# An S4D block and a routed feed-forward, one core: the mixer laid out by channel, its power tables expanded on GpSimd, its group outputs passed through a DRAM table

## The chip, the cores and the metric

The kernel runs on one core of a Trainium2 chip. TensorE (PE), VectorE (DVE), ScalarE (ACT), GpSimd (POOL) and SyncE (SP, which here issues DMAs) run their own instruction streams and wait for each other by semaphores. The metric is the device time of one launch in microseconds (us), as the median of several runs. A profile of one execution has its own span, from the first instruction to the last.

## The reference

All data are fp32: 8 batches of 512 tokens with 128 features, 256 mixer channels, 8 complex states for each channel.

```python
xz = einsum('bld,ed->bel', hidden, W_in);  x, z = split(xz, 2, axis=1)
x = silu(causal_depthwise_conv(x, conv_w, 4 taps) + conv_b)
A = -exp(log_A_real) + 1j * A_imag;  dtA = exp(log_dt) * A
Ct = (C_re + 1j * C_im) * (exp(dtA) - 1) / A
k = 2 * real(einsum('hn,hnl->hl', Ct, exp(dtA * t)))        # t = 0 .. 511
y = causal_convolution(x, k) + x * D                        # by FFT
h = layernorm(hidden + einsum('bhl,dh->bld', y * silu(z), W_out))
e = argmax(h @ gate_w.T + gate_b + expert_bias)             # 1 of 8 experts
out = layernorm(h + relu(h @ w1[e] + b1[e]) @ w2[e] + b2[e])  # 128 -> 512 -> 128
```

Both kernels do the long convolution in 4 chunks of 128 tokens. Inside a chunk, a channel's x is multiplied by a 128x128 Toeplitz matrix of k. From chunk to chunk, 8 complex states (16 numbers) for each channel are carried forward and multiplied by powers of exp(dtA). The 256 channels are worked through in 32 groups of 8.

## The kernel before

The program has four stages.

**Projection and tables (0 to 80 us).** The four convolution taps are folded into four copies of the input weights (`Wx`), so PE projects x with four accumulated matmuls for each chunk (L1292) and the gate input z with one (L1275). DVE adds the bias and writes x into `X`, where a channel's values lie 128 bytes apart (L881); ACT copies z into `Z` (L643). Beside this ACT and DVE build the power tables: `turnsC` and `Ctab`, made by whole-table arithmetic over 2048 columns (L982, L983, exponentials at L659, sines), and the lag tables `Btab` and `decay`. PE sums the rows of k, SP writes them to a DRAM table and reads Toeplitz matrices back. SP also fills the whole DRAM table of routed rows with empty rows in this stage (three DMAs of 2310 KB and one of 1848 KB).

**Groups (80 to 131 us).** For each of 32 groups PE convolves (L1370), sums the states that enter each chunk (L1357), transposes the output of the group before back to tokens in partitions and adds its states (L1380, L1384). ACT copies x and the PSUM results for it (L713, L719, L723), DVE masks states (L1044) and multiplies the output by the gate (L1057, straight out of PSUM into `X`). POOL multiplies `Btab` with `decay` for each group (`group_tables`, L515); of both tables it takes one group's column, and the group index is the innermost of 32, so that an input row is read at a step of 128 bytes. SP streams one 512 KB Toeplitz block per group through 8 slots (L424).

**Output projection and routing (131 to 142 us).** PE transposes the gated output (L1418), ACT copies it (L761), PE multiplies by the output weights (L1433, L1435). Then come squares and the deviation on ACT, the routing of each batch ("quad") on DVE, and the place of each token. Constants for these are written by POOL at L586 to L597. POOL then sends each tile of 128 rows to its place in the DRAM table (`dispatch`, L568).

**Experts (142 to 264 us).** 32 indirect dispatches by POOL; after the first 20 SP begins to load slots (L450); 39 expert blocks on PE (L1469, L1477, L1487), each with its weights from SP (L371), its layernorm on DVE and ACT and an indirect store by POOL (L576).

What orders the work is the written order on each engine and the semaphores; there is no planner.

## Time and profile before

| | us |
|---|---|
| time, median of 3 runs (lowest, highest) | 269.08 (268.27, 269.29) |
| span of the profiled execution | 263.8 |
| stage of projection and tables | 0 to 80 |
| stage of the groups | 80 to 131 |
| output projection up to the first dispatch | 131 to 141.9 |
| from the first dispatch to the end | 141.9 to 263.8 |

The profiled execution has no run time of its own on record, only its span. The launch's time contains the span and what lies around it: the median is 5.3 us above the span. PE is busy for 91% of the span, DVE 67%, ACT 71%, POOL 53%. These shares are means over stages with different limits, so the stages are to be read one by one.

### The profile page before, as it was taken

How to read it: one execution, taken by the hardware profiler on the slowest of the kernel's cores; microseconds unless marked ns; L12 is line 12 of the kernel's file. 1: busy time of each engine (PE TensorE's matmuls, PEld its weight loads, DVE VectorE, ACT ScalarE, POOL GpSimd, SP SyncE). 2: the span in 40 equal slices, each digit the busy share in tenths (PEclk: the TensorE clock that was granted, in tenths of full speed). 3: DMA queues.
4: the chain of work that ended last, by engine and by line, in shares of the span. 5: the costliest groups of instructions: out<-in, count | busy, mean ns of one | idle time of the engine just before them, and what ended most of it. 6: DMA issues, size and time to landing. Idle time of an engine off the chain costs nothing.

```text
span 263.8 us, 8892 instructions
## 1 busy us (share of the span) xinstructions
PE 239.2 (91%) x2763; PEld 215.1 (82%) x2764; DVE 177.0 (67%) x552; ACT 187.1 (71%) x528; POOL 139.8 (53%) x208
## 2 busy tenths in 40 slices
PE   8999979999999899999979999359989999999970
PEld 4888768888887678888869999349979999899960
DVE  1889995997218657777724878842877676566672
ACT  2999999856998778888655665207667777667740
POOL 6000000400009989999624687878746656657545
PEclk9999999999999999999999999759999999999995
DMA  7697884600399999999293221647865676677600
GB/s 232 180 313 288 346 334 150 244 0 0 105 310 332 310 279 296 308 320 302 66 361 120 93 93 41 212 92 191 220 179 172 200 210 164 203 195 208 189 34 6
DMA packets 54267, 52.06 MB, mean 197 GB/s; under 512 B 4415, under 2 KB 42817, under 8 KB 54114
## 3 DMA queue, kind: packets, MB, share of 16 engines
q1 hardware_dynamic: 51506, 46.65, 59.2%
q0 software_dynamic: 2304, 4.34, 4.6%
q10 hardware_dynamic: 432, 0.79, 0.8%
q8 instruction: 11, 0.18, 0.3%
q14 instruction: 14, 0.11, 0.1%
HBM read 38.14 MB, written 14.07 MB: 198 GB/s over the span
## 4 chain that ended last, share of the span: by engine, by line
PE 59%; DVE 10%; ACT 10%; POOL 9%; issue 6%; DMA 5%; SPq 1%; DVEq 0%; ACTq 0%; POOLq 0%
PE banks L1292 13%; PE banks L1477 9%; PE banks L1487 8%; PE banks L1370 7%; POOL dispatched_rows L568 5%; ACT BR L672 5%; PE banks L1380 5%; PE banks L1384 4%; PE banks L1275 3%; PE banks L1357 3%; PE banks L1435 2%; DMA X<-dispatched_rows 2%; POOL RE L558 1%; DMA out<-X 1%; POOL out L576 1%
## 5 line engine op out<-in xcount | busy, mean ns | idle before, releaser
L515 POOL TENSOR_TENSOR Wx<-BR,RE 128x384 f32 (+1 forms) x32 | 47.9, 1548 | 27.9 <-PE banks L1292 26.6
L1292 PE MATMUL banks<-Wx,XT 128*128 128x256 f32 x256 | 59.9, 380 | 1.7 <-ACT Z L643 1.7
L809 ACT ACTIVATE Z<-banks,BR 128x128 f32<-128x128 f32 x156 | 44.6, 368 | 18.4 <-PE banks L1477 18.3
L1292 PEld LDWEIGHTS banks<-Wx,XT 128*128 128x128 f32 x256 | 48.4, 190 | 9.0 <-issue 2.2
L576 POOL DMA_INDIRECT out<-X x39 | 38.4, 986 | 27.8 <-DVE X L1233 15.3
L1477 PE MATMUL banks<-Z 128*128 128x128 f32 x312 | 42.7, 281 | 0.4 <-ACT Z L798 0.2
L1487 PE MATMUL banks<-BR,Z 128*128 x312 | 41.1, 276 | 1.2 <-DVE X L1216 1.2
L1477 PEld LDWEIGHTS banks<-Z 128*128 128x128 f32 x312 | 39.0, 196 | 1.0 <-issue 0.5
L1487 PEld LDWEIGHTS banks<-BR,Z 128*128 128x128 f32 x312 | 37.8, 192 | 1.5 <-issue 1.5
L568 POOL DMA_INDIRECT dispatched_rows<-TR,CR x32 | 31.0, 970 | 9.3 <-POOL RE L558 9.3
L1057 DVE TENSOR_TENSOR X<-banks,Z 128x256 f32 (+1 forms) x32 | 20.4, 636 | 9.1 <-PE banks L1384 9.1
L521 POOL MEMSET RE<- 128x128 f32 x1 | 0.2, 205 | 44.0 <-DVE CR L989 44.0
L1370 PE MATMUL banks<-TR,RE 128*32 128x128 f32 x512 | 21.3, 279 | 1.4 <-issue 1.2
L1216 DVE TENSOR_TENSOR X<-banks,X 128x128 f32<-128x128 f32 x39 | 11.3, 289 | 14.9 <-PE banks L1487 13.4
L881 DVE TENSOR_TENSOR X<-banks,cbias 128x512 f32<-128x512 f32 x15 | 15.3, 1062 | 8.5 <-PE banks L1275 8.4
L1435 PE MATMUL banks<-Wx,RE 128*128 128x136 f32 x128 | 20.1, 279 | 0.0
L1370 PEld LDWEIGHTS banks<-TR,RE 128*32 128x32 f32 x512 | 12.3, 109 | 9.4 <-ACT RE L713 5.8
L798 ACT ACTIVATE Z<-banks 128x128 f32<-128x128 f32 x39 | 11.3, 289 | 10.8 <-PE banks L1469 10.3
L1275 PE MATMUL banks<-Win,XT 128*128 128x256 f32 x64 | 18.5, 381 | 0.0
L772 ACT ACTIVATE RE<-banks 128x128 f32<-128x128 f32 x32 | 8.9, 278 | 13.2 <-PE banks L1435 8.8
L558 POOL MEMSET RE<- 128x128 f32 x56 | 12.7, 226 | 9.1 <-DVE CR L1141 7.9
L1044 DVE SCALAR_TENSOR_TENSOR Win<-banks,RE,mask 128x192 f32<-128x192 f32 x32 | 13.4, 418 | 6.1 <-PE banks L1357 4.3
(220 smaller groups left out, 469.6 us busy)
## 6 DMA issues: line engine op xcount, KB each, us to landing
TR<-kernel_rows SPq DMA_DIRECT2D x32, 512.0 KB, 6.5
Z<-w SPq DMA_DIRECT2D x39, 256.0 KB, 3.1
dispatched_rows<-TR SPq DMA_DIRECT2D x3, 2310.0 KB, 8.8
X<-dispatched_rows SPq DMA_DIRECT2D x39, 66.0 KB, 2.1
XT<-hidden_t SPq DMA_DIRECT2D x10, 256.0 KB, 3.1
RE<-decay_and_turns SPq DMA_DIRECT2D x2, 1024.0 KB, 7.4
BR<-w SPq DMA_DIRECT2D x1, 2048.0 KB, 8.2
dispatched_rows<-TR SPq DMA_DIRECT2D x1, 1848.0 KB, 7.8
```

What stands on the lines that cost most here:

```text
L515: nc.gpsimd.tensor_tensor(BC[:, k, 0:LAGS, :].rearrange("p m (s r n) -> p (m s) r n", s=STRIPS, r=2), Btab[:, :, :, :, :, one].rearrange(" ...
L558: nc.gpsimd.memset(pause[:, 0:columns], 0.0).then_inc(s_pause, 1)
L568: pool.indirect_dma_start(slots_dram, bass.IndirectOffsetOnAxis(pos[:, batch, k:k + 1], 0), X1[:, batch, k, :], None).then_inc(s_sc[batch] ...
L576: pool.indirect_dma_start(out_rows, bass.IndirectOffsetOnAxis(XS[:, n % ROWS_RING, TOKEN_COL:TOKEN_COL + 1].bitcast(U32), 0), F[:, slot, : ...
L809: last = nc.scalar.activation(HT[:, j, c * P:c * P + P], bank[UP_BANKS[j]][:, c * P:c * P + P], ACT.Relu, bias=B1[:, bass.ds(experts[j] * ...
L1057: tt(group, bank[4 + k][:, 0:GH * TILES].rearrange("p (h t) -> p h t", h=GH), gates, ALU.mult).then_inc(s_yc, 1)
L1275: return mm(bank[Z_BANKS[k]][:, j * CHAN:(j + 1) * CHAN], XT[:, slot, at:at + CHUNK], Win[:, CHAN:], start=True, stop=True)
L1292: last = mm(bank[X_BANKS[k]][:, j * CHAN:(j + 1) * CHAN], XT[:, slot, at:at + CHUNK], Wx[:, tap, :], start=(tap == 0), stop=(tap == TAPS - 1))
L1370: last = mm(yt[part:part + TILES, at:at + P], xg[:, h, :], Tring[:, k, h, :], start=True, stop=True)
L1435: last = mm(projected(slot, k), GT[:, slot, k, j * P:j * P + P], Wo[:, j, :], start=False, stop=(j == 1))
L1477: last = mm(bank[UP_BANKS[m % 4]][:, c * P:c * P + P], WS[:, stage, c * P:c * P + P], XsT[:, m % DEEP, :], start=True, stop=True)
L1487: last = mm(bank[DOWN_BANKS[m % 2]][:, 0:P], HT[:, m % DEEP, c * P:c * P + P], W2[:, e, c * DM:(c + 1) * DM].rearrange("p e d -> p (e d)") ...
```

## The change

The mixer is laid out anew.

- x is projected by channel: PE makes 16 units (2 halves of 128 channels, 8 batches) of 128 channels by 512 tokens, and 16 like it for z, which ACT passes through Silu into `Z`. The taps are no longer in the weights: ACT applies the last tap and the bias (`last_tap`), DVE the other three in one instruction each (`add_taps`), PE transposes a unit (`turn_x`) and ACT writes it through Silu into `X` (`keep_x`).
- The power tables are built from 16 fine and 8 coarse angles for each channel and state. DVE, ACT and POOL make the short tables (896 columns and small ones of 32). POOL then expands them into the full 128x2048 halves of `Etab`, by two products and one sum each (`expand_half`), and makes the turning matrices (`turning`). The second product of each half goes into `products`, which lies in the upper half of `X`.
- For each four groups PE sums the local states (`sum_local`), ACT copies them, PE turns them by the lags (`turn_states`), DVE masks them; for each group PE convolves into an output bank and adds the states there as two halves of 64 rows (`add_states`). The transposes of the group output and `group_tables` are gone.
- ACT copies a group's output (`keep_y`) and sends it from its own DMA queue (`send_y`, 128 KB) into the DRAM table `rows_dram`. SP reads the table back into `Y` in three loads (`LOADS`: groups 0 to 15, 16 to 27, 28 to 31), four partitions for each group and 32 KB for each partition, so that channels lie in partitions again by chunk and batch.
- The gate is a product of `Y` and `Z` over 1024 columns for each quad: quads 0, 2, 4, 6 and 7 on DVE, 1, 3 and 5 on POOL. `Y` goes straight into the output projection; its transposes and copies are gone, and hidden states are all held, so the four late loads of them are gone.
- Toeplitz slots go from 8 to 5. The early fills of empty rows are gone; instead SP writes 8 blocks of 66 KB behind the experts' last rows, ahead of the slot loads of block 8.

The core of the diff:

```diff
-T_SLOTS = 8
...
+T_SLOTS = 5
...
+POOL_QUADS = (1, 3, 5)
+LOADS = ((0, 16), (16, 28), (28, 32))
...
+        def expand(engine, out, part, by_coarse, by_fine):
+            count = part.stop - part.start
+            shape = [P, count, COARSE, FINE]
+            return engine.tensor_tensor(
+                out.rearrange("p g (b a) -> p g b a", b=COARSE), by_coarse[:, part, :].unsqueeze(3).to_broadcast(shape),
+                by_fine[:, part, 0:FINE].unsqueeze(2).to_broadcast(shape), ALU.mult)
+
+        def gate(engine, n):
+            y, z = [a[:, n * CHUNKS:(n + 1) * CHUNKS, :, :].rearrange("p t j u -> p (t j u)") for a in (Y, Z)]
+            return engine.tensor_tensor(y, y, z, ALU.mult)
...
+            def store_rows(j):
+                sp.wait_ge(s_kx, 2 * j + 2)
+                sp.dma_start(kext[j * P:(j + 1) * P, :], Kx[:, j, :]).then_inc(s_kd[j], 16)
+                sp.wait_ge(s_kd[j], 16)
...
+            store_rows(0)
+            for g in range(T_SLOTS):
+                load_toeplitz(g)
+            store_rows(1)
+            def load_outputs(k):
+                first, end = LOADS[k]
+                for slot in range(Y_RING):
+                    sp.wait_ge(s_yd[slot], end // Y_RING * 16)
+                sp.dma_start(Y[first * 4:end * 4, :, :, :].rearrange("p t j u -> p (t j u)"), rows_dram[first * 4:end * 4, :])\
+                    .then_inc(s_yl[k], 16)
+
+            for g in range(T_SLOTS, 24):
+                load_toeplitz(g)
+            load_outputs(0)
+            for g in range(24, GROUPS):
+                load_toeplitz(g)
+            load_outputs(1)
...
+                if g == EARLY_BLOCKS - 4:
+                    sp.wait_ge(s_last, 2)
+                    sp.wait_ge(s_ends, 2)
+                    starts = table_values(sp, ends, 0, EMPTY_ROW - P) + table_values(sp, ends, 4, EMPTY_ROW - P)
+                    for downwards in range(2):
+                        wait_past(sp, s_fill, downwards * 16 * (EXPERTS // 2))
+                        for e in range(downwards, EXPERTS, 2):
+                            sp.dma_start(slots_dram[bass.ds(starts[e], P), :], empty_block).then_inc(s_fill, 16)
...
-            def group_tables(r, k):
-                g = r * 2 + k
-                wait_apart(pool, s_s, g - 1)
-                one = bass.ds(g, 1)
...
-                nc.gpsimd.tensor_tensor(
-                    BC[:, k, 0:LAGS, :].rearrange("p m (s r n) -> p (m s) r n", s=STRIPS, r=2),
-                    Btab[:, :, :, :, :, one].rearrange("p m s r n g -> p (m s) r (n g)"),
...
+            def turning(part):
+                count = (part.stop - part.start) * LAGS * 2
+                tt(Rot[:, part, :].rearrange("p g (m c) -> p (g m) c", c=FINE),
+                   turned[:, part, :, :].rearrange("p g m r -> p (g m r)").unsqueeze(2).to_broadcast([P, count, FINE]),
+                   same_state[:, :].unsqueeze(1).to_broadcast([P, count, FINE]), ALU.mult).then_inc(s_rot, 1)
+
+            def expand_half(part, ready):
+                expand(nc.gpsimd, Etab[:, part, :], part, first_coarse, cosine)
+                done(expand(nc.gpsimd, products[:, part, :], part, second_coarse, sine))
+                tt(Etab[:, part, :], Etab[:, part, :], products[:, part, :], ALU.add).then_inc(ready, 1)
+
+            pool.wait_ge(s_far, 1)
+            expand_half(slice(0, HALF), s_e0)
+            turning(slice(0, HALF))
+            expand_half(slice(HALF, GROUPS), s_e1)
+            turning(slice(HALF, GROUPS - HALF // 2))
+            turning(slice(GROUPS - HALF // 2, GROUPS))
...
-            pool.wait_ge(s_yc, GROUPS + LEAD)
+            for k in range(len(LOADS) - 1):
+                pool.wait_ge(s_yl[k], 16)
+            pool.wait_ge(s_yl[-1], 16)
+            pool.wait_ge(s_z, UNITS)
+            for n in POOL_QUADS:
+                gate(nc.gpsimd, n).then_inc(s_gp, 1)
             nc.gpsimd.memset(OH[:, :, :, 4], 0.0)
...
+            def last_tap(u):
+                j = u // BATCH
+                act.wait_ge(s_x, u + 1)
+                wait_past(act, s_xtr, u - 1)
+                nc.scalar.activation(xc[:, u % 2, :], bank[u % 2], ACT.Identity,
+                                     scale=channel[:, j, TAPS - 1:TAPS], bias=channel[:, j, TAPS:TAPS + 1]).then_inc(s_x3, 1)
+
+            def keep_x(u):
+                j, b = u // BATCH, u % BATCH
+                act.wait_ge(s_xtr, u + 1)
+                nc.scalar.activation(x_chunks[:, j * P:(j + 1) * P, b, :], bank[2][:, :].rearrange("p (k c) -> p c k", k=CHUNKS),
+                                     ACT.Silu).then_inc(s_xe, 1)
...
+            def keep_y(g):
+                act.wait_ge(s_y, g + 1)
+                wait_past(act, s_yd[g % Y_RING], g // Y_RING * 16)
+                nc.scalar.activation(YT[:, g % Y_RING, :].rearrange("p (j u) -> p j u", j=2), later_first(g),
+                                     ACT.Copy).then_inc(s_yt, 1)
+
+            def send_y(g):
+                act.wait_ge(s_yt, g + 1)
+                home = rows_dram[g * 4:g * 4 + 4, :].rearrange("h (t c) -> (h t) c", t=TILES)
+                act.dma_start(home, YT[:, g % Y_RING, :]).then_inc(s_yd[g % Y_RING], 16)
...
+            act.wait_ge(s_rot, 1)
+            keep_local(0)
+            act.wait_ge(s_e1, 1)
+            keep_x(8)
+            last_tap(10)
+            for n in range(TURNS):
+                keep_y(4 * n)
+                if n:
+                    send_y(4 * n - 1)
+                if n + 1 < TURNS:
+                    keep_local(n + 1)
+                if n == 0:
...
+            def add_taps(u):
+                j = u // BATCH
+                dve.wait_ge(s_x3, u + 1)
+                for back in range(1, TAPS):
+                    if back > 1:
+                        dve.wait_ge(s_xk, u * LAGS + back - 1)
+                    stt(xc[:, u % 2, back:], bank[u % 2][:, 0:SEQ - back], channel[:, j, TAPS - 1 - back:TAPS - back],
...
+            def gate_quad(n):
+                if n < QUADS and n not in POOL_QUADS:
+                    gate(nc.vector, n).then_inc(s_gd, 1)
+
+            for k in range(len(LOADS)):
+                dve.wait_ge(s_yl[k], 16)
+            dve.wait_ge(s_z, UNITS)
+            gate_quad(0)
+            gate_quad(2)
             dve.wait_ge(s_cconst, 2)
             dve.wait_ge(s_oc, 2)
             dve.wait_ge(s_rconst, 1)
...
+            def convolve(g):
+                halves = output_banks(g)
+                pe.wait_ge(s_t[g % T_SLOTS], (g // T_SLOTS + 1) * 16)
+                wait_past(pe, s_yt, g - 1)
+                for h in range(GH):
+                    part = h % 4 * TILES
+                    last = mm(halves[h // 4][part:part + TILES, 0:P], X[:, g * GH + h, :], Tring[:, g % T_SLOTS, h, :],
+                              start=True, stop=False)
+                last.then_inc(s_tm, 1)
+
+            def add_states(g):
+                halves = output_banks(g)
+                pe.wait_ge(s_v, g + 1)
+                for j in range(2):
+                    rows = slice(j * 64, (j + 1) * 64)
+                    last = mm(halves[j][:, 0:P], V[rows, g % V_RING, :, :].rearrange("p h t -> p (h t)"), Etab[rows, g, :],
+                              start=False, stop=True)
...
+                        mm(projected(slot, k), XT[:, batch, at], centre[:, :], start=True, stop=False)
+                        if n in POOL_QUADS:
+                            pe.wait_ge(s_gp, POOL_QUADS.index(n) + 1)
+                        else:
+                            pe.wait_ge(s_gd, n + 1 - len([q for q in POOL_QUADS if q < n]))
                         for j in range(2):
-                            last = mm(projected(slot, k), GT[:, slot, k, j * P:j * P + P], Wo[:, j, :], start=False,
-                                      stop=(j == 1))
+                            last = mm(projected(slot, k), Y[:, batch * CHUNKS + k, j, :], Wo[:, j, :],
+                                      start=False, stop=(j == 1))
```

Three places in the order of instructions, each first as it was and then as it is. Names are those of the program's buffers; some hold one thing after another (`CR` first `Etab`, `EN` first the small tables and then `YT`, `X` in its upper half first `products`).

ACT at the start of the groups, before: copies of x and of a group's results alternate, and none waits for a table.

```order
L643 ACTIVATE Z<-banks 128x2x32x8 [waits last_gates_projected]
L713 ACTIVATE RE<-X 128x256 [waits x_biased]
L738 ACTIVATE Z<-Z 128x512 [waits z_ready,silu_table_loaded]
L719 ACTIVATE Wx<-CR 128x128
L723 ACTIVATE RE<-banks 128x256 [waits toeplitz_multiplied]
L713 ACTIVATE RE<-X 128x256 [waits states_summed]
L719 ACTIVATE Wx<-CR 128x128 [waits group_done]
```

The same place on ACT after the change:

```order
L718 ACTIVATE EN<-banks 128x192 [waits local_states_summed,turning_matrices_ready]
L693 ACTIVATE X<-banks 128x128x4 [waits x_transposed,second_half_powers_ready]
L687 ACTIVATE xc<-banks,channel 128x512 [waits x_transposed,x_projected]
L724 ACTIVATE EN<-banks 128x256 [waits group_done]
L718 ACTIVATE EN<-banks 128x192 [waits local_states_summed]
L706 ACTIVATE Kx<-banks 128x127 [waits kernel_rows_summed,constants_ready]
L707 ACTIVATE Kx<-banks,channel 128x1
L712 ACTIVATE ET<-banks 128x512 [waits powers_transposed]
L724 ACTIVATE EN<-banks 128x256 [waits group_done]
L730 DMA group_outputs<-EN 128x256 [waits group_output_copied]
```

Unit 8 of x is now kept (L693) only when POOL has the second half of the powers; the first group's output (L724) and the second half of the kernel's rows (L706) stand behind it.

POOL ahead of the groups, before: constants, then a group's tables at a time.

```order
L535 MEMSET RE 128x1
L536 MEMSET RE 128x40
L538 IOTA RE 128x40x4 x2
L541 IOTA RE 128x40
L515 TENSOR_TENSOR Wx<-BR,RE 128x384 [waits state_decay_ready,state_sines_ready,projection_ready]
L515 TENSOR_TENSOR Wx<-BR,RE 128x384
```

There after the change, behind 31 small instructions:

```order
L345 TENSOR_TENSOR CR<-Y 128x2048 [waits coarse_powers_ready,state_pattern_ready,pool_step]
L345 TENSOR_TENSOR X<-Y 128x2048
L585 TENSOR_TENSOR CR<-CR,X 128x2048 [waits pool_step]
L578 TENSOR_TENSOR Rot<-EN,same_state 128x1536
L345 TENSOR_TENSOR CR<-Y 128x2048
L345 TENSOR_TENSOR X<-Y 128x2048
L585 TENSOR_TENSOR CR<-CR,X 128x2048 [waits pool_step]
L578 TENSOR_TENSOR Rot<-EN,same_state 128x768 x2
L594 MEMSET EN 128x128 [waits turning_matrices_ready]
```

The first seven of these rows stand ahead of the signal that L693 waits for on ACT.

POOL between the groups and the routing, before:

```order
L580 MEMSET Win 128x128
L583 AFFINE_SELECT Win<-Win 128x128 [waits counting_constants_ready]
L586 MEMSET RE 128x16 [waits mixer_output_copied]
L587 MEMSET RE 128x40
L589 MEMSET RE 128x8 [waits one_hot_constants_ready]
L590 MEMSET CR 128x1
L591 MEMSET CR 128x1
L592 MEMSET TR 128x32x3
```

The same place after the change:

```order
L645 MEMSET Win 128x128 [waits gates_projected,x_projected]
L648 AFFINE_SELECT Win<-Win 128x128 [waits counting_constants_ready]
L351 TENSOR_TENSOR Y<-Y,Z 128x1024 [waits outputs_loaded2,gates_ready,outputs_loaded1,outputs_loaded0]
L351 TENSOR_TENSOR Y<-Y,Z 128x1024 x2
L656 MEMSET EN 128x16
L657 MEMSET EN 128x40
L659 MEMSET EN 128x8 [waits one_hot_constants_ready]
L660 MEMSET CR 128x1
L661 MEMSET CR 128x1
L662 MEMSET TR 128x32x3
```

Three gates now stand ahead of the constants. DVE waits for these constants behind its own first two gates:

```order
L351 TENSOR_TENSOR Y<-Y,Z 128x1024 [waits outputs_loaded2,gates_ready,outputs_loaded1,outputs_loaded0]
L351 TENSOR_TENSOR Y<-Y,Z 128x1024
L1117 MEMSET rs 128x4 [waits one_hot_constants_ready,dispatch_constants_ready,counting_constants_ready]
L1119 TENSOR_SCALAR EN<-EN 128x8 [waits residual_added_to_block]
L1120 TENSOR_SCALAR CR<-EN 128x8
L1121 TENSOR_SCALAR EN<-EN 128x8
L351 TENSOR_TENSOR Y<-Y,Z 128x1024 [waits vector_step]
L1003 RECIPROCAL rs<-sd 128x4 [waits deviation_ready]
```

The routing chain of the first quad (L1003) comes behind the wait at L1117 and behind DVE's third gate.

## Rows read from the trace of the kernel before

**Rows 1.** The page's span and its chain that ended last, by engine.

```profile
span 263.8 us, 8892 instructions
...
PE 59%; DVE 10%; ACT 10%; POOL 9%; issue 6%; DMA 5%; SPq 1%; DVEq 0%; ACTq 0%; POOLq 0%
```

**Rows 2.** Busy time by stretch: PE, PEld, DVE, ACT, POOL; clock, DMA share, GB/s.

```profile
34.00:80.00 46.00, 45.56 (x264) 39.60 (x264) 31.15 (x33) 38.67 (x49) 4.06 (x17) 1.00 0.50 169
...
80.00:131.00 51.00, 49.26 (x1417) 40.10 (x1418) 35.83 (x68) 41.76 (x114) 47.50 (x34) 1.00 0.98 279
```

**Rows 3.** The chain in order of time: start, us, what.

```profile
0.82 3.00 DMA RE<-states
...
36.37 0.43 PE banks L1275 x2
...
120.78 0.57 PE banks L1370 x16
...
122.25 0.57 PE banks L1370 x16
...
142.88 0.88 PE banks L1418 x8
```

**Rows 4.** Timeline between the last group and the first dispatch.

```profile
130.43 0.60 DVE L1057 TENSOR_TENSOR X<-banks,Z 128x256 f32<-128x256 f32 x1
...
137.44 0.18 DVE L1085 RECIPROCAL rs<-sd 128x4 f32<-128x4 f32 x1 [4.39 <-ACT sd L781]
...
141.89 0.96 POOL L568 DMA_INDIRECT dispatched_rows<-TR,CR  x1 [0.50 <-POOL RE L558]
```

**Rows 5.** Instructions by form, POOL: busy and mean ns of one | idle before.

```profile
L515 POOL TENSOR_TENSOR Wx<-BR,RE 128x384 f32 x30 | 44.9, 1549 | 1.3 <-PE banks L1357 1.2
...
L499 POOL MEMSET TR<- 128x1024 f32 x1 | 1.0, 952 | 0.0
...
L497 POOL TENSOR_TENSOR mask<-mask 128x8 f32<-128x8 f32 x1 | 0.2, 200 | 0.1
```

**Rows 6.** The same view, DVE.

```profile
L881 DVE TENSOR_TENSOR X<-banks,cbias 128x512 f32<-128x512 f32 x15 | 15.3, 1062 | 8.5 <-PE banks L1275 8.4
...
L1122 DVE TENSOR_TENSOR TR<-banks,rs 128x512 f32<-128x512 f32 x8 | 5.3, 665 | 0.0
...
L1057 DVE TENSOR_TENSOR X<-banks,Z 128x256 f32 x30 | 19.1, 638 | 8.7 <-PE banks L1384 8.7
...
L983 DVE TENSOR_TENSOR BR<-BR 128x2064 f32<-128x2064 f32 x2 | 4.6, 2310 | 0.1
```

**Rows 7.** The same view, ACT.

```profile
L643 ACT ACTIVATE Z<-banks 128x512 f32<-128x512 f32 x16 | 9.1, 585 | 3.9 <-PE banks L1275 3.9
...
L723 ACT ACTIVATE RE<-banks 128x256 f32<-128x256 f32 x32 | 12.3, 384 | 5.3 <-PE banks L1370 5.0
...
L704 ACT ACT_TABLE_LOAD x1 | 1.3, 1283 | 0.0
```

**Rows 8.** DMA issues: count, KB of one, median us from issue to landing.

```profile
TR<-kernel_rows SPq DMA_DIRECT2D x32, 512.0 KB, 6.5
...
X<-dispatched_rows SPq DMA_DIRECT2D x39, 66.0 KB, 2.1
...
BR<-w SPq DMA_DIRECT2D x1, 2048.0 KB, 8.2
```

**Rows 9.** Timeline of SP's DMA queue, in the groups and among the experts.

```profile
82.30 39.89 SPq L424 DMA_DIRECT2D TR<-kernel_rows  x24
...
183.51 0.33 SPq L371 DMA_DIRECT2D Z<-w  x1
...
184.67 0.33 SPq L450 DMA_DIRECT2D X<-dispatched_rows  x1
```

**Rows 10.** Timeline among the experts, PE and POOL.

```profile
189.75 0.27 PE L1469 MATMUL banks<-ident,X 128*128 128x128 f32 x1
...
207.58 0.98 POOL L576 DMA_INDIRECT out<-X  x1 [0.79 <-POOL RE L558]
```

More of the change, by code:

```diff
@@ L194, in build @@
         cnt = late(400, 6 * KINDS).rearrange("p (i e) -> p i e", e=KINDS)
+        ends = late(344, EXPERTS, I32)
+        last_used = late(352, EXPERTS)
+        behind = late(360, EXPERTS)
         erow = EN[:, 2192:2200]
@@ L746, in _ @@
[L746 to L762 removed]
+            act.wait_ge(s_falls, 1)
@@ new lines, in _ @@
+            for i in range(6):
+                keep_z(i)
+            keep_x(0)
+            last_tap(2)
+            keep_z(6)
+            keep_z(7)
+            keep_x(1)
+            last_tap(3)
+            for i in range(8, 12):
+                keep_z(i)
+            for u in range(2, 6):
+                keep_x(u)
+                last_tap(u + 2)
+                keep_z(u + 10)
+            keep_x(6)
+            last_tap(8)
+            keep_rows(0)
+            keep_powers(0)
+            keep_powers(1)
@@ L1311, in _, with group @@
+            def group(g):
+                convolve(g)
+                add_states(g)
             pe.wait_ge(s_warm, 1)
             for j in range(WARMING):
[L1313 to L1318 removed]
```

1158 lines of the change are left out of this document (514 added, 644 removed).

## The prediction

> **What bounds the kernel now.** I read the chain that ended last first: 59% of it is PE, and no other engine has more than 10% [rows 1]. Then the busy time by stretch, because the stages differ. In 34 to 80 us PE works for 45.6 of 46 us while the DMAs are half idle: the projection, with its taps in the weights, is PE's. In 80 to 131 us PE (49.3), POOL (47.5) and the DMAs (share 0.98) are all nearly full [rows 2]; the chain runs through the convolutions at one group in 1.47 us (120.78 to 122.25) [rows 3]. A change that frees PE alone gets little there. The third place is the gap from the last group's gated output to the first dispatch, 131.03 (130.43 + 0.60) to 141.89, thus 10.86 us [rows 4]. From there to the end it is 263.8 − 141.89 = 121.9 us. So the time of the changed kernel is settled by when its first dispatch starts, if nothing behind it changes. I build that time up from zero.
>
> **To the start of the expansions.** The changed kernel gives POOL the power tables: two products and a sum of 2048 columns for each half, with a turning of 1536 between them. Ahead of them stand: the five parameter rows, landed at 3.8 [rows 3]; two exponentials, 0.5, and two small products, 0.4; DVE's angles, five passes over 896 columns, of which the two-input ones cost 2310/2064 = 1.12 ns a column [rows 6], about 4.8 with the cheaper one-input ones: 9.8. A table load for the sines, 1.28 [rows 7], and the sines, 0.9: 12.0. On DVE then some small ones, the taps of the first unit (3 × 0.7, from 665 ns for 512 columns out of PSUM [rows 6]) and two decay products, 3.0 together: 15.0. On POOL 15 small operations of about 0.27 (200 ns for 8 columns [rows 5]; these have 32) with waits between, 4.5, then the selector (256 columns) and six of 96, 3.7: the expansions start at **23.2**.
>
> **The expansions.** Up to the signal for the second half, which ACT waits for before it keeps unit 8 of x, POOL passes 6 × 2048 + 1536 = 13,824 columns. With r ns for a column this ends at 23.2 + 13.8r. No row shows POOL on a two-input operation with inputs side by side, so r is bounded. From above: L515, 1549/384 = 4.03, which reads at a step of 128 bytes. From below: the memset, 952/1024 = 0.93, which reads nothing [rows 5]. What does such a step cost? On DVE L881, which writes at that step, takes 1062 against 665 for as many columns, 1.6 times; L1057, 638 for 256 columns, is 1.9 times as dear a column [rows 6]. With 1.75, halfway, L515 without its step is 4.03/1.75 = 2.3. I take **r = 2.3**, nearer to L515 because that is the same kind of instruction: the signal at 55.0. The Trainium skill, page GPSIMD Engine Reference, § 3.1 (side-by-side cycle accounting), gives 4497 ns for such an addition of 2048 fp32 columns, against 2293 ns on DVE; the DVE figure agrees with L983's 2310 here, and no run here shows the other. By it r is 2.2 and the total 276.
>
> Is POOL what the groups wait for? Unit by unit, the x path has PE for two projections of 512 columns (0.43 for 256 [rows 3], so 0.86 each) and four transposes (0.11 each, from 0.88 for 8 [rows 3]), 2.2; DVE 2.1 and ACT three passes of 585 [rows 7]. Units 0 to 7, the early powers and local sums make it ready at 38 to 45, I take 42. So POOL is later by 13, and the whole queue behind ACT's wait is late: the first group's output, the second half of k's rows, and with these SP's Toeplitz loads from the sixth on.
>
> **From the signal to the end of the groups.** First PE's leftovers: seven transposed units, five or six projections, rows and transposes of the second half, 14.3 us, between twelve groups of 1.2 (less than the 1.47 of before, without transposes), and 3 of passing back and forth: 32 us to the end of group 11. Meanwhile the sixth Toeplitz load can go only at 5.2 behind the signal (ACT's four operations, 2.6, and the store of k's rows, 0.35 + 2.1 + issue [rows 8]). Then the DMAs lead: 39.89/24 = 1.66 us for 512 KB [rows 9], at a DMA share that was already 0.98 [rows 2]; each group now also sends 128 KB, up to 0.42 by size, of which I take 0.3 since ACT's queue fills gaps. Loads 15 to 31 are 17 × 1.96 = 33.3, the first of them lands after 6.5 [rows 8], the last group takes 2.1. Sum: 32 + 33.3 + 6.5 + 2.1 = 74: **129.0**. Bounds: 64, if the loads run at their own pace from the sixth on; 78, if sends cost in full and the ring of 5 (was 8) adds its latency.
>
> **Group outputs by way of DRAM.** Before, the last output was in place once DVE had gated it. Now: copy 0.5, two sends' issue 0.9, store 2.1 and issue 0.4, and the third load, 16 partitions of 32 KB. For that, 3.8 if the partition count doesn't matter; the nearest row, 2048 KB into 128 partitions in 8.2 [rows 8], moves half as much in each partition, so 16.4 would be the bound. I take 3.8, since only 512 KB remain when the other two loads lie behind. In all **8** to 21: landed at 137.
>
> **Gates and routing.** POOL now runs three gates of 1024 columns before it writes the constants that DVE's chain for the first quad waits for: 3.07r = 7.1. I charge them whole, because the chain of that quad stands behind that wait on DVE. Then constants 1.2, DVE's third gate 1.15 (1024 × 1.12 [rows 6]), and from the reciprocal to the dispatch as before, 141.89 − 137.44 = 4.45 [rows 4]: **6.8**. First dispatch at 137 + 7.1 + 6.8 = **150.9**, 9.0 later. What is saved (transposes, copies, and POOL's tables per group) is within these numbers: the whole is 23.2 + 74 + 8 + 6.8 + 16.9r = 112 + 16.9r, equal to 141.89 at **r = 1.77**.
>
> **The early fills go, others come.** The old fills ran beside the projection, where the DMA share was 0.50 [rows 2]: no gain. The new ones, eight DMAs of 66 KB in two waves, stand on SP before the slot of block 8: each wave has four issues of 0.33 [rows 9] and 2.1 to land [rows 8], with reads of their addresses about 8.5 together. That slot is loaded at 184.67 [rows 9] and needed when block 8 opens, 189.75 [rows 10], so 5.1 of it lies in SP's lead and 3.5 would be late. POOL's stores trail the blocks there (block 8's at 207.58 [rows 10]), and that backlog hides it: I take 0, bound 3.5.
>
> So the profiled time is 263.8 + 9.0 = 272.8, and with the 5.3 between span and median, taken as it was, **278**.
>
> **The rivals.** *POOL is fast* (the other side). If r lies near the memset, the expansions end before the x path and the groups start at 42; that is r = 1.36. The first dispatch comes at 42 + 74 + 8 + 6.8 + 4.2 = 135, 6.9 earlier: **262**; at 0.93 1.3 less, at r = 1.6 it is 266. For it: POOL's two products read inputs that repeat one value or a row of 16, with no large step. Against it: two reads and a write for each column, where the memset only writes. It decides below 1.77. Chance 0.20; near 1.77, no change, 0.07.
>
> *POOL is as slow as L515 shows.* r = 4.03: 112 + 68.1 = 180.1, 38 later, **307**. For it: the only row of its kind. Against it: the step of 128 bytes, which costs DVE 1.6 to 1.9. Chance 0.10.
>
> *Loads into few partitions are slow.* At half the rate for the 64 and 48 partitions the three loads cost about 11 more, **289**. For it: 32 KB in each partition, twice as much as in the expert weights' load that took 8.2 [rows 8]. Against it: the first two have groups to hide behind. The Trainium skill, page SBUF — State Buffer, § "Door 1: The DMA port swizzle", says that partitions 0 to 63 reach only half of the 16 ports; no row here shows it, and by its figures the loads would add an estimated 6, 284. Chance 0.13.
>
> **How the numbers follow.** The forecast has 0.50, with its own range of 272 to 287 (r from 2.0 to 2.6 is ±5, the group phase −10 to +4, of which part is shared). All slower cases: 0.50 + 0.10 + 0.13 = 0.73; faster 0.20; the same, within 0.5%, about what a measurement of this kernel can tell from no change, 0.07. The range goes down to 263, into the fast case, and up to 300, past the slow loads but short of 307.
>
> **What the changed profile would show.** POOL's L345 at 4.7 us for 2048 columns, its first near 23; ACT's L693 ended by POOL at about 55; PE waiting for ACT before that; Toeplitz loads at 1.9 to 2.0 us each afterwards; the last load landing near 137 and the first dispatch at 151, with DVE's L1117 ended by POOL; behind it 122 us. The prediction is wrong if L345 is under 3.5 us, if PE's wait at the second half ends by something else than POOL, if the Toeplitz loads keep 1.66 or less, or if the experts' part is not 122.

## The result, and the profile after

The changed kernel takes 302.09 us (299.61 to 308.17, 5 runs) against 269.08: 1.1215 times as long, 95% interval 1.1142 to 1.1289. That is slower, as forecast, but 33 us instead of 9, and 2 us beyond the range. Of a second launch of the same kernel (301.0 us) the trace is used here, because the first one was taken in a run with PE's clock lower than in the others. The run of this second trace took 300.68 us by its own time and 298.9 by its span, so only 1.8 us lies around a span; most of the 5.3 us that I put there is the distance of the profiled run of before from the median.

The page of the second trace, span and chain by engine, answers to [rows 1]:

```profile
span 298.9 us, 8238 instructions
...
PE 45%; POOL 23%; DMA 14%; issue 10%; DVE 3%; ACT 3%; SPq 2%; ACTq 0%; POOLq 0%; DVEq 0%
```

POOL, the DMAs and "issue" (nothing that the profile shows is waited for) took what PE lost. The timeline of POOL's expansions, and of ACT where it waits for them:

```profile
21.95 3.67 POOL L345 TENSOR_TENSOR CR<-Y 128x2048 f32<-128x2048 f32 x1
...
43.97 4.53 POOL L585 TENSOR_TENSOR CR<-CR,X 128x2048 f32<-128x2048 f32 x1
...
48.53 0.60 ACT L693 ACTIVATE X<-banks 128x512 f32<-128x512 f32 x1 [7.26 <-POOL CR L585]
```

They start at 22.0 and end at 48.5: 26.5 us for 13,824 columns, r = 1.92. SP's DMA queue, to be read against [rows 9]:

```profile
52.77 48.16 SPq L410 DMA_DIRECT2D TR<-kernel_rows  x19
101.11 0.60 SPq L420 DMA_DIRECT2D Y<-group_outputs  x1
102.31 23.55 SPq L410 DMA_DIRECT2D TR<-kernel_rows  x8
...
132.24 14.93 SPq L420 DMA_DIRECT2D Y<-group_outputs  x2
```

A Toeplitz load every 2.5 us (48.16/19), then 2.9 behind the first load of outputs, where it was 1.66. That pace is PE's, not the DMAs': SP waits 45.0 us in all, in 25 waits, for PE to be done with a slot, while PE waits for a Toeplitz load 1.3 us in all between the signal and the end of the groups. The DMA issues (count, KB, median us to landing), to be read against [rows 8]:

```profile
TR<-kernel_rows SPq DMA_DIRECT2D x32, 512.0 KB, 6.1
group_outputs<-EN ACTq DMA_DIRECT2D x32, 128.0 KB, 4.7
...
Y<-group_outputs SPq DMA_DIRECT2D x1, 2048.0 KB, 15.4
Y<-group_outputs SPq DMA_DIRECT2D x1, 1536.0 KB, 14.1
```

The expert weights' load of 2048 KB took 8.2 [rows 8]; the same bytes into 64 partitions take 15.4. By stretch (columns as in [rows 2]), the DMAs' share is 0.78 at 115 GB/s in 140 to 150, in which the second load ends and the third begins, where in the groups before it was 0.98 at 279:

```profile
110.00:120.00 10.00, 3.26 (x37) 2.07 (x40) 0.00 (x0) 0.76 (x2) 0.00 (x0) 0.54 0.96 263
...
140.00:150.00 10.00, 0.00 (x0) 0.00 (x0) 0.00 (x0) 0.00 (x0) 0.00 (x0) 0.50 0.78 115
```

In 110 to 120 PE works for 3.26 of 10 us. Its timeline there:

```profile
107.47 0.64 PE L1280 MATMUL banks<-TR,X 128*32 128x128 f32 x15
...
116.74 0.37 PE L1280 MATMUL banks<-TR,X 128*32 128x128 f32 x1 [8.63 <-issue]
```

PE stops for 8.6 us between the two recorded halves of one matmul of a convolution (8 matmuls leave 16 records), which is no place to wait for data. From the last group to the first dispatch, to be read against [rows 4]:

```profile
132.93 0.38 ACT L724 ACTIVATE EN<-banks 128x256 f32<-128x256 f32 x1 [1.45 <-PE banks L1289]
...
153.74 4.51 DVE L351 TENSOR_TENSOR Y<-Y,Z 128x1024 f32<-128x1024 f32 x2 [29.37 <-DMA Y<-group_outputs]
...
153.77 8.98 POOL L351 TENSOR_TENSOR Y<-Y,Z 128x1024 f32<-128x1024 f32 x3 [81.57 <-DMA Y<-group_outputs]
...
163.52 0.06 DVE L1117 MEMSET rs<- 128x4 f32 x1 [5.26 <-POOL TR L663]
163.96 1.22 DVE L351 TENSOR_TENSOR Y<-Y,Z 128x1024 f32<-128x1024 f32 x1
...
169.91 0.96 POOL L631 DMA_INDIRECT dispatched_rows<-TR,CR  x1 [0.49 <-POOL ET L621]
```

From the last copy to the landed outputs it is 20.4 us (133.3 to 153.7). The chain that ended last shows what fills them (start, us, what):

```profile
133.34 13.44 DMA group_outputs<-EN
146.85 6.70 DMA Y<-group_outputs
```

The last sends, 128 KB each, need 13.4 us beside the second load (issued at 132.2, landed at 146.3), and the third load can be issued only behind them, at 146.9. POOL's gates take 9.0, DVE's two beside them 2.26 each and the one alone 1.22; the first dispatch is at 169.9. Among the experts the late fills stand on SP's queue for 7.3 us ahead of block 8's slot:

```profile
214.84 7.32 SPq L465 DMA_DIRECT2D dispatched_rows<-ET  x8
223.14 0.35 SPq L443 DMA_DIRECT2D Z<-dispatched_rows  x1
```

### The profile page after: what moved, and what is told of

The parts are those of the page before. It is cut to its first block, busy times and chain, and to the rows that moved or that the text cites. A ratio compares the mean times of both kernels' runs of the same rounds, so it can differ in the third digit from the quotient of the medians.

```text
span 306.4 us, 8238 instructions
## 1 busy us (share of the span) xinstructions
PE 225.6 (74%) x2787; PEld 179.5 (59%) x2788; DVE 143.2 (47%) x484; ACT 129.5 (42%) x402; POOL 144.7 (47%) x221
## 4 chain that ended last, share of the span: by engine, by line
PE 37%; POOL 20%; DMA 14%; issue 13%; DVE 9%; ACT 3%; SPq 2%; ACTq 0%; POOLq 0%; DVEq 0%
PE banks L1280 8%; PE banks L1446 6%; PE banks L1289 6%; POOL out L639 4%; DMA group_outputs<-EN 4%; PE banks L1456 4%; POOL CR L585 3%; POOL Y L351 3%; PE banks L1270 3%; PE banks L1208 3%; POOL CR L345 2%; POOL X L345 2%; DMA Z<-dispatched_rows 2%; DMA XT<-hidden_t 2%; DMA Y<-group_outputs 2%
## 5 line engine op out<-in xcount | busy, mean ns | idle before, releaser
L864 ACT ACTIVATE Z<-banks,CR 128x128 f32<-128x128 f32 x156 | 44.6, 369 | 20.2 <-PE banks L1446 20.2
L639 POOL DMA_INDIRECT out<-Z x39 | 38.6, 989 | 28.7 <-POOL ET L621 12.7
L1456 PE MATMUL banks<-X,Z 128*128 x312 | 41.9, 279 | 0.0
L914 DVE SCALAR_TENSOR_TENSOR xc<-banks,channel,xc 128x511 f32<-128x511 f32 (+2 forms) x48 | 35.7, 748 | 13.1 <-ACT xc L687 11.9
L1456 PEld LDWEIGHTS banks<-X,Z 128*128 128x128 f32 x312 | 38.6, 196 | 0.0
L1408 PE MATMUL banks<-Wox,Y 128*128 128x136 f32 x128 | 23.1, 309 | 19.9 <-DVE Y L351 19.9
L1280 PE MATMUL banks<-TR,X 128*32 128x128 f32 x512 | 26.8, 338 | 10.4 <-issue 8.6
L724 ACT ACTIVATE EN<-banks 128x256 f32<-128x256 f32 x32 | 12.3, 384 | 48.9 <-PE banks L1289 36.1
L1408 PEld LDWEIGHTS banks<-Wox,Y 128*128 128x128 f32 x128 | 20.1, 218 | 20.2 <-DVE Y L351 20.2
L1289 PEld LDWEIGHTS banks<-CR,EN 64*128 64x128 f32 x128 | 13.4, 246 | 22.8 <-issue 22.0
L1289 PE MATMUL banks<-CR,EN 64*128 64x128 f32 x128 | 21.6, 412 | 3.4 <-issue 3.4
L1208 PE MATMUL banks<-XT,Win 128*128 128x512 f32 x32 | 20.7, 736 | 2.6 <-DMA XT<-hidden_t 2.6
L1147 DVE TENSOR_TENSOR Z<-banks,Z 128x128 f32<-128x128 f32 x39 | 11.4, 292 | 17.1 <-PE banks L1456 16.4
```

The source lines that it names most:

```text
L639: pool.indirect_dma_start(out_rows, bass.IndirectOffsetOnAxis(XS[:, n % ROWS_RING, TOKEN_COL:TOKEN_COL + 1].bitcast(U32), 0), F[:, slot, : ...
L724: nc.scalar.activation(YT[:, g % Y_RING, :].rearrange("p (j u) -> p j u", j=2), later_first(g), ACT.Copy).then_inc(s_yt, 1)
L864: last = nc.scalar.activation(HT[:, j, c * P:c * P + P], bank[UP_BANKS[j]][:, c * P:c * P + P], ACT.Relu, bias=B1[:, bass.ds(experts[j] * ...
L914: stt(xc[:, u % 2, back:], bank[u % 2][:, 0:SEQ - back], channel[:, j, TAPS - 1 - back:TAPS - back], xc[:, u % 2, back:], ALU.mult, ALU.ad ...
L1208: mm(bank[u % 2], Win[:, j * P:(j + 1) * P], XT[:, b, :], start=True, stop=True).then_inc(s_x, 1)
L1280: last = mm(halves[h // 4][part:part + TILES, 0:P], X[:, g * GH + h, :], Tring[:, g % T_SLOTS, h, :], start=True, stop=False)
```

## The experiments

**The kernel as it is**, for the trace above.

> The changed kernel as it is, to have a trace and a time beside the next three. First trace: powers' signal at 51.1 us, last group output 141.0, last load of the outputs landed 160.5, first dispatch 176.7. Every theory expects about 300 us and these four places within a few us (the granted clock was 0.5 to 0.7 in much of 100 to 160 us, so PE's part may vary).

Measured: 301.0 us; signal 48.5, last copy ended 133.3, outputs landed 153.7, first dispatch 169.9. The four places are 2.6 to 7.7 us earlier than in the first trace, and the distances behind the groups are the same within 1 us.

**Loads into 128 partitions.**

```diff
-sp.dma_start(Y[first * 4:end * 4, ...], rows_dram[first * 4:end * 4, :])
+count = (end - first) * 4 * 2 * TOKENS // P
+sp.dma_start(y_flat[:, first * 256:first * 256 + count],
+             bass.AP(rows_dram[:, :].tensor, first * 4 * 2 * TOKENS, [[count, P], [1, count]])).then_inc(s_yl[k], 16)
```

> The three loads of the group outputs carry the same bytes at the same places in the program, but into all 128 partitions (16, 12 and 4 KB for each) instead of 64, 48 and 16 partitions of 32 KB; the outputs come back in another layout, so the result is another one. Theory 1 (a load into few partitions moves 32 KB through each at a fixed pace, 15.6 us for the first in the first trace, and holds up the Toeplitz loads and the sends meanwhile): the first load takes some 8 us, the stall of 8.6 us of PE at 114 us goes, the last two loads take 8 instead of 19; together 15 to 20 us less than the changed kernel. Theory 2 (the DMAs simply have 8 MB more to move, however it is laid out): within 3 us of the changed kernel.

Measured: 286.16 us, 15 less, the first dispatch at 153.6. The loads in this kernel, as a DMA view:

```profile
Y<-group_outputs SPq DMA_DIRECT2D x1, 2048.0 KB, 10.8
Y<-group_outputs SPq DMA_DIRECT2D x1, 1536.0 KB, 7.0
```

PE's longest stop is 3.7 instead of 8.6, so it shrinks but does not go, and the last sends take 6.1 instead of 13.4. Theory 2 falls.

**The same rows into every second partition.**

```diff
+where = ((0, 128), (1, 97), (97, 128))[k]
-sp.dma_start(Y[first * 4:end * 4, ...], rows_dram[first * 4:end * 4, :])
+sp.dma_start(y_flat[where[0]:where[1]:2, :], rows_dram[first * 4:end * 4, :])
```

> The changed kernel with its three loads as they were (64, 48 and 16 rows of 32 KB, each into a partition of its own, at the same places in the program), only the partitions are others: every second one from 0, every second one from 1 to 95, every second one from 97, so the result is another one. What the run with 128 partitions left open is told apart. Theory 1a (32 KB through one partition is what takes the time): the first load still takes 15 us and the whole is within 2 us of the changed kernel, 299 to 301. Theory 1b (what counts is which partitions are written: the Trainium skill, page SBUF, has partitions 0 to 63 on half of the 16 ports, and partitions spread over both halves on all): the first two loads take 8 to 11 us, as with 128 partitions, and the whole is 10 to 15 us faster.

Measured: 291.66 us, 9 less (some 7 by the ratios to the kernel before, 1.095 against 1.1196), the first dispatch at 159.2:

```profile
Y<-group_outputs SPq DMA_DIRECT2D x1, 2048.0 KB, 11.0
Y<-group_outputs SPq DMA_DIRECT2D x1, 1536.0 KB, 9.2
```

Just as many partitions and 32 KB in each, and 4 to 5 us less for each of the two large loads (into 128 partitions it was 5 and 7 less): which partitions are written is what counts most. That agrees with the rule of the Trainium skill (SBUF — State Buffer, § "Door 1: The DMA port swizzle") that partitions 0 to 63 reach half of the ports. Theory 1a falls; theory 1b has the loads right and sizes the whole (10 to 15 us) a little too high. The last sends take 8.6 us here.

**The first load behind the Toeplitz loads.**

```diff
-load_outputs(0)
 for g in range(24, GROUPS): load_toeplitz(g)
+load_outputs(0)
 load_outputs(1)
```

> The first load of the group outputs is issued behind the last Toeplitz load instead of eight ahead of it; nothing else changes. Theory 1 (a load into few partitions is slow and shares nothing with the others): the groups end some 9 us earlier, without the stall of PE at 114 us, but the first load's 15 us then comes after them in part, so the first dispatch is within 4 us of the changed kernel. Theory 2 (only bytes count): also no change, but the last loads together then last 13 us for 4 MB rather than over 20.

Measured: 302.65 us, first dispatch 171.0. PE's stop of 8.6 us is 2.6 here, at the same matmul, but the last sends now wait behind the load, as ACT's timeline shows:

```profile
123.25 0.38 ACT L724 ACTIVATE EN<-banks 128x256 f32<-128x256 f32 x1 [1.11 <-DMA group_outputs<-EN]
133.13 0.38 ACT L724 ACTIVATE EN<-banks 128x256 f32<-128x256 f32 x1 [9.49 <-DMA group_outputs<-EN]
```

So the groups end no earlier (134.0), against theory 1, which had the load sharing nothing with the others: it holds up the sends, as it held up PE before. The last sends again need 14.1 us beside the second load. The three loads take 15.0, 14.1 and 6.5 us, so it is not their bytes (4 MB in 13 us, theory 2).

**Half of the second expansion left out.**

```diff
-expand_half(slice(HALF, GROUPS), s_e1)
+expand(nc.gpsimd, Etab[:, HALF:, :], slice(HALF, GROUPS), first_coarse, cosine).then_inc(s_e1, 1)
```

> POOL leaves out the second product and the sum of the second half of the powers, so the second half is half computed. The signal that ACT waits for comes 8.2 us earlier, at about 43. My step (the groups wait for POOL, and everything behind is a fixed distance from the signal): the whole is 8 us faster, less what the x path's own end (local sums copied at 42.6 in the first trace) keeps back. Rival (the groups are a matter of the DMAs, which are not full before 80 us): under 3 us faster, because DMA work from 80 us on is the same.

Measured: 300.91 us in the median (296.1 to 302.85), no difference that could be told from the spread; in the trace the first dispatch is 2.8 us earlier (167.1). POOL gives the signal at 40.7, but ACT now waits for PE:

```profile
45.85 0.60 ACT L693 ACTIVATE X<-banks 128x512 f32<-128x512 f32 x1 [4.70 <-PE banks L1223]
```

The x path is ready at 45.9, so POOL was the last by 2.7 us only (48.5 before). My step falls by size, and the rival's bound of 3 us holds; that does not show its reason, the DMAs.

**All gates on DVE** (`POOL_QUADS = ()`, gates 0 to 2 ahead of the constants).

> All eight gates on DVE (three ahead of the first quad, then one ahead of each), none on POOL; the rest is the changed kernel. In its trace POOL's three gates took 8.98 us, 3.0 each, and the two that DVE ran beside them 2.26 each, while DVE's later ones alone took 1.14. Theory 1 (DVE and POOL hold each other up when both read two operands of SBUF, and DVE's chain waits for POOL): DVE's gates take 1.14 each from the start, and from the landing of the last load to the first dispatch it is 10 us instead of 16.1; 5 to 6 us faster. Theory 2 (a gate has its price on either engine, 2.3 to 3.0): DVE's three take 6.8, and the whole is within 2 us.

Measured: 299.86 us, no difference in time; from the landing to the first dispatch it is 12.3 us instead of 16.2. All eight gates take 1.2 us on average:

```profile
L351 DVE TENSOR_TENSOR Y<-Y,Z 128x1024 f32<-128x1024 f32 x8 | 9.5, 1220 | 29.4 <-DMA Y<-group_outputs 29.4
```

So DVE's 2.26 was POOL's presence (theory 1), but the gain was sized too large: 3.9 us instead of 6 behind the landing, where PE's clock was as low as before (0.64 against 0.61). The whole shows none of it in this trace, because the groups ended 3.9 us later (137.2 instead of 133.3).

**Early fills** (the late block removed; four DMAs of empty rows beside the projection).

> The eight late fills are gone; the whole table is filled with empty rows beside the projection, as in the kernel before, from a part of the Toeplitz buffer that DVE writes first. Theory 1 (the late fills, 7.3 us on SP's queue, hold up the slots from block 8 on; POOL's store backlog does not cover it): from the first dispatch to the end it is 5 us less than 129. Theory 2, that of my prediction (the backlog of stores covers it): under 1 us. The fills themselves should cost nothing early, where the DMAs move nothing from 8 to 38 us, unless they delay the first Toeplitz loads at 38.5.

Measured: 297.35 us. From the first dispatch to the end it is 295.9 − 171.3 = 124.6 us instead of 129.0: theory 1, 4.4 us in this pair of traces.

**Sends doubled.**

```diff
 act.dma_start(home, YT[:, g % Y_RING, :]).then_inc(s_yd[g % Y_RING], 16)
+act.dma_start(again, YT[:, g % Y_RING, :]).then_inc(s_yd[g % Y_RING], 16)
```

> Each group's output is sent twice, the second time into a table that nobody reads. Theory 1 (in the groups the DMAs are the bound, so that each send costs what it takes of the 16 engines, 0.4 us): the 20 groups from the twelfth on take 8 us longer, 3% of the whole. Rival (sends fill gaps that the 5 Toeplitz slots and PE leave): under 3 us.

Measured: the ratio to before is 1.1516 (1.1389 to 1.1643) where the kernel as it is has 1.1196 (1.1106 to 1.1286): 3%, some 8 us, the size of theory 1. That the DMAs are the bound, its reason, is not shown by this: in this trace PE waits for Toeplitz loads 4.0 us in all, where it was 1.3.

**Where PE stops.** In all nine traces up to here, of kernels with the same code on PE, PE stopped after the same 959, 1210, 1336 and 1587 recorded matmuls. Empty instructions were to move the places:

> The changed kernel with 64 empty instructions on PE ahead of the first group, where PE waits for POOL's powers anyway. Theory 1 (PE's instructions come in blocks, and a block that is late behind the other transfers stops PE): the stops of 1.5 to 9 us move to 32 recorded matmuls earlier, 927, 1178, 1304 and 1555 instead of 959, 1210, 1336 and 1587, and keep their distances. Theory 2 (these matmuls wait for data): they stay at the same matmuls. The time is the changed kernel's, about 300.

This told nothing: the trace has the same 8238 instructions as the changed kernel's, so the empty ones are not in the program, and it was the changed kernel once more (304.99 us, stops at the same counts). Small matmuls took their place:

```diff
 pe.wait_ge(s_z, UNITS)
+for _n in range(32):
+    mm(bank[6][:, 0:32], ident[:, :], ident[:, 0:32], start=True, stop=True)
```

> The changed kernel with 32 small matmuls of no use (32 columns) on PE ahead of the first group's convolution, where PE waits for POOL's powers anyway; they go into a bank that the second group overwrites. Theory 1 (PE's instructions come in blocks, and a block that is late behind the other transfers stops PE): the stops stay at the same counts of recorded matmuls, 959, 1210, 1336 and 1587 with the dummies counted, so that they hit other matmuls of the groups, as many records earlier in the program as the dummies have. Theory 2 (certain matmuls wait for data): the stops stay with their matmuls, and the counts rise by the dummies' records, 32 or 64. The time is about that of the changed kernel, 299 to 303.

Measured: 308.96 us in the one run, more than expected (ACT keeps unit 8 of x 6.3 us later, at 54.9, because PE's x path is late); the dummies are 64 records. The stretches from 0 to a stop, with PE's records counted, first of the kernel as it is:

```profile
0.00:78.75 78.75, 67.18 (x959) 39.03 (x960) 48.97 (x86) 47.65 (x86) 49.85 (x80) 0.98 0.50 147
...
0.00:108.14 108.14, 90.46 (x1587) 55.83 (x1589) 51.62 (x100) 53.24 (x101) 49.85 (x80) 0.91 0.61 176
```

and with the dummies:

```profile
0.00:83.05 83.05, 75.94 (x960) 47.95 (x961) 48.02 (x82) 47.14 (x85) 50.02 (x80) 0.94 0.44 130
...
0.00:114.42 114.42, 101.36 (x1588) 66.30 (x1589) 50.88 (x96) 52.94 (x100) 50.02 (x80) 0.88 0.58 165
```

The counts stay (960, 1212 and 1588; after 1336 there is no stop here) and the matmuls change; 1588 now falls among the turned states:

```profile
113.76 0.63 PE L1270 MATMUL banks<-EN,Rot 32*32 32x48 f32 x48
117.98 0.63 PE L1270 MATMUL banks<-EN,Rot 32*32 32x48 f32 x48 [3.58 <-issue]
```

So PE waits for instructions, not for data (theory 1). The distance between stops is 126 recorded matmuls or twice that, thus 252 instructions with the weight loads. With PE's semaphore instructions counted too, the five stops of the kernel as it is lie 513, 255, 511 and 513 records apart, which is 256 or twice 256 within one.

The trace holds the transfers of these blocks themselves. They have a DMA queue of their own, here as the page of the kernel as it is lists it (packets, MB, share of 16 engines):

```profile
q8 instruction: 19, 0.31, 0.4%
```

Each packet has 16,384 bytes. PE went on 1.3 to 1.5 us after such a packet had ended, at each of the five stops; for the stop of 8.6 us the packet ran from 114.1 to 115.4, and PE from 116.7. With the dummies the three stops named end 1.4 to 1.6 us after a packet. (Another long stop there, 3.6 us after 1656 records, is a wait for ACT.) The Trainium skill (Runtime: NRT & Kernel Launch, § Instruction fetch mechanics) says that instructions are refilled in blocks of 256 by DMA, "mostly hidden"; the first part agrees with this trace, the second does not: here five of the eight crossings between 78 and 133 us stop PE, four of them for 1.5 to 3 us beside full DMA queues and one for 8.6 beside the slow load.

**Outputs by quads.**

```diff
+LOADS = ((0, 1), (1, 2), (2, 4), (4, 8))          # quads, all partitions, behind the last group
...
+sp.dma_start(Y[:, first * CHUNKS:end * CHUNKS, ...], rows_dram[:, first * CHUNKS * 256:end * CHUNKS * 256])
...
-for n in POOL_QUADS: gate(nc.gpsimd, n)           # POOL waits for the last group alone
```

> The group outputs come back by quads behind the last group (quad 0, quad 1, quads 2 and 3, quads 4 to 7: all 128 partitions, 4 to 16 KB for each, at a pitch of 32 KB), each gate waits for its own load alone, all gates are on DVE, and POOL writes its constants as soon as the last group is done. Theory 1 (few partitions and the order of loads cost 8.6 us in the groups and 12 behind them, the gates on POOL another 9): the groups end near 124 instead of 133, the first quad lands some 6 us later, the first dispatch stands at about 138 to 140 instead of 170, and the whole is about 30 us faster than the changed kernel, about as fast as the one before. Theory 2 (bytes count, not partitions): the groups end at about 127, the table's 4 MB takes 13 us, the first dispatch at 150 or later.

Measured: 278.03 us, 23 less than the changed kernel, first dispatch at 145.9. Theory 1, short by 6 to 8 us. The last sends now take 1.8 us, with no load beside them; but from the end of the first gate to the dispatch it still takes 11 us, with PE's clock at 0.52 in 130 to 140.

**Quads and early fills.**

> Outputs by quads behind the groups, gates on DVE, and the fills of empty rows early. The two gains were 24 us (298.9 to 274.8 in span) and 4.4 us (first dispatch to the end). If they add up: about 273.5 us, 2% slower than the kernel before. If the early fills get into the way of what the quads made early, over 276.

Measured: 273.91 us, as expected. The ratio to the kernel before, run beside each, falls from 1.0387 to 1.0279 and the part behind the first dispatch from 128.9 to 126.0 us: some 3 us of the 4.4.

**13 Toeplitz slots**, eight of them in `Y` until the outputs come.

> The run above, with 13 Toeplitz slots instead of 5: four more in the part of the outputs' buffer that nothing uses before the loads, and four in the part that is free when the powers are expanded. Theory 1 (the DMAs are the bound from 80 us on, because with 5 slots they stand still before: share 0 from 8 to 38 us, 0.7 from 50 to 80): loads run ahead of PE, the groups end at 105 to 110 instead of 127, and the whole takes about 255, faster than both kernels. Rival (PE with its clock at half, and the wait of each group for its neighbours, would take as long anyway): within 5 us of the run above.

Measured: 271.9 us in the median of four runs (268.53, 269.83, 273.96, 274.5), 2 to 5 less, and not 255. The loads run ahead (DMA share 1.0 to 1.15 from 50 to 80 us) and the last copy ends at 121.9 instead of 128.2, but PE, which never waits for a Toeplitz load here, needs that long, so the rival is nearer. The quads then start at half clock, here by stretch:

```profile
130.00:140.00 10.00, 6.88 (x33) 6.67 (x32) 6.01 (x18) 1.77 (x9) 0.31 (x2) 0.67 1.03 437
```

**PE kept busy in the pause.**

```diff
 pe.wait_ge(s_yt, GROUPS)
+for _n in range(8):
+    mm(bank[0][:, :], ident[:, :], XT[:, 0, :], start=True, stop=True)
```

> The run with 13 slots, with eight matmuls of no use on PE between the last group and the first quad (8 times 0.86 us at full clock), and the outputs loaded in five pieces instead of four, so that the third quad's gate does not wait for the fourth quad's bytes. In that run the granted clock was 0.67 in 130 to 140 us and four matmuls took 0.91 instead of 0.46. Theory 1 (PE's pause of 7 us is why its clock is at half in the first quads): the clock is 1.0 there, the first dispatch 2 to 3 us earlier, the second quad without its gap, the whole 3 to 5 us faster, 267 to 269, the same as the kernel before. Rival (the chain there is ACT's and DVE's): under 1 us.

Measured: 266.41 us against 267.76 of before, 0.9917 times (0.986 to 0.9975): as fast as the kernel before, or faster by a little. The same stretch:

```profile
130.00:140.00 10.00, 6.88 (x45) 6.39 (x44) 7.38 (x23) 2.12 (x11) 1.12 (x2) 0.88 1.04 436
```

Theory 1 in part: the clock is 0.88 there and not 1.0, four matmuls of the first quad take 0.63 us where most took 1.11 or more, and from the first gate to the first dispatch it is 9.9 us instead of 12.1. The five loads changed with it, and the groups ended 1.5 us later in this trace, so the rest of these 5 us is not shown to be the clock's.

## Why the prediction was wrong, step by step

The direction held: group outputs by way of DRAM, ahead of a dispatch that everything behind waits for, cost more than the work they replace. Measured against forecast (second trace, us):

| term | forecast | measured |
|---|---|---|
| start of the expansions | 23.2 | 22.0 |
| signal for the second half | 55.0 | 48.5 |
| signal to the end of the groups | 74 | 84.8 |
| groups' end to the landed outputs | 8 | 20.4 |
| POOL's three gates | 7.1 | 9.0 |
| from there to the first dispatch | 6.8 | 7.2 |
| first dispatch | 150.9 | 169.9 |
| first dispatch to the end | 121.9 | 129.0 |

- *The expansions.* r was 1.92, not 2.3: 1.79 for the products, 2.2 for the sum. Either L515's step costs POOL more than the 1.75 that I took from DVE, or DVE's work beside it did, as with the gates; no run tells these apart. (The parts ahead add up to 9.5 where I wrote 9.8.)
- *"So POOL is later by 13."* This step failed. The x path is ready at 45.9, not 42, and POOL at 48.5: 2.7. The whole sum 112 + 16.9r leans on r where little hung on it; the rival of a fast POOL would have had the groups start at 45.9 and not at 42, where the x path stops it, thus 266 by its own sum instead of 262.
- *"From the signal to the end of the groups", 74.* This step failed in its mechanism. "Then the DMAs lead" is not what the trace shows: PE leads, and waits for Toeplitz loads 1.3 us in all. The sum lacked PE's instruction fetch: five stops of 16.2 us in all, 8.6 of them beside the first load. The kernel before ran its groups in a loop and shows one stop of 0.95. Without the stops it would be 68.6; that this is near 74 is luck, since the terms were others. Sends cost about their bytes by the run that doubles them (8 us for 20 groups).
- *"I take 3.8, since only 512 KB remain."* This is the step that failed by most. The second load did not lie behind: it was issued at 132.2 and needed 14.1 us, and the last sends, "store 2.1", needed 13.4 beside it (1.8 in the run by quads, where no load is under way). Only then could the third load go, and it took 6.7. That 20.4 lies within my bound of 21 is luck, since that bound had the third load alone at 16.4. The rival of slow loads had the right mechanism, with a chance of 0.13, but not its path: it priced the loads themselves (11; measured 12.4 more, mostly as a wait for the sends), and not that the load in the midst would stop PE.
- *Gates.* 2.95 ns a column on POOL and 2.26 us on DVE, which ran at once; 1.2 us on DVE alone. POOL's gates alone were not run.
- *Fills, "I take 0, bound 3.5".* 4.4 by the run with early fills, 2.9 in the pair by quads; POOL's backlog hid little or nothing. Of the rest of the 7.1 us more in the experts' part, 2.1 go with the second quad's late start (the 32 dispatches last 48.7 instead of 46.5 us from first to last); that this is the cause is argued, not shown.

The terms ahead of the first dispatch add up: −6.5 + 10.8 + 12.4 + 1.9 + 0.4 = 19.0 us. Of the prediction's own signs of being wrong only the last one came, the experts' part; the two terms that failed by most had no sign among them.

What stays open: how much of the groups' time is the half clock. PE's granted clock is 0.5 (1.2 of 2.4 GHz) in 80.1 to 86.9, 93.7 to 103.9 and 110.8 to 121.0, stretches that begin during a stop or up to 1.3 us behind one. A group takes 1.74 us there and 1.00 at full clock, so that an estimate from these rows is 8 us for the 18 in which PE works.

## What to carry to other kernels

Ask of each load which partitions it writes, not only how many bytes: 2 MB spread over both halves, or over all 128, came in 11 us where 64 neighbours took 15. Ask too what else moves meanwhile: a small store that others wait for took 13 us beside such a load and 2 without. Unrolled code on a busy engine is itself DMA traffic: look in the timeline for stops inside a run of equal instructions, at whether they keep their count from kernel to kernel, and at when the packets of the instruction queue end. A term that hangs on "X is later than Y" wants both times sized with care, for past the crossing its slope is gone.

## What was unexpected of the hardware

- PE stops at fixed counts of instructions, 256 or a multiple apart, for 1.5 to 8.6 us while the DMA share is 0.87 to 1.1, longest beside a load into half of the partitions, and goes on 1.3 to 1.5 us after a 16 KB packet of the instruction queue.
- Sends of 128 KB take 13.4 us beside a load of 1.5 MB into 48 neighbouring partitions, 8.6 when these are every second one, 6.1 when it goes into all 128, and 1.8 with no load beside them.
- DVE's product of two SBUF operands takes 2.26 us for 1024 columns beside POOL's and 1.22 alone, while POOL's column costs 2.95 ns beside DVE's product and 1.79 to 2.2 in the expansions.
- After 7 us without work PE's granted clock stands at 0.52 to 0.67 in 130 to 140 us (two levels, 1.2 and 2.4 GHz, mixed); with eight matmuls of no use in the pause it is 0.88.
